# A vision tower's first batch: its mixer is put in front of the class token's set-up

## What is computed

```python
ek = exp(k); ew = exp(w_bias * local_mask)              # token mixer, q, k, v = 1x1 projections of x
y  = sigmoid(q) * (ew @ (ek * v)) / (ew @ ek)
h  = layernorm(y @ out_w + out_b + x) * ln_g + ln_b
h  = concat([cls_tok, h])                               # 257 tokens
W_ = amp * cos(phase)                                   # per q, k, v, o; 32 harmonics, 16 heads of 16
h  = h + holo(attention(layernorm(h)))                  # each projection: (z @ basis.T) @ W_.T
h  = h + ffn(layernorm(h))                              # shared and 8 routed experts, top 2
```

## Time and profile before

| | |
|---|---|
| median of 3 runs (lowest, highest) | 2409.51 us (2408.36, 2416.81) |
| profiled execution: its time, its span | 2408.09 us, 2406.3 us |
| TensorE busy, share of the span | 2203.2 us, 92% |
| VectorE, ScalarE, GpSimd busy | 59%, 42%, 28% |
| mean granted TensorE clock | 0.981 |

### The profile page before, as it was taken

How to read it: one execution, slowest core, us unless ns; L and a number is a source line. 1 busy time by engine, 2 the same in 40 slices (tenths; PEclk the granted TensorE clock), 3 DMA queues, 4 the chain that set the end, 5 groups by cost and what they waited for, 6 DMA issues and landing times. The chain is left out here.

```text
span 2406.3 us, 42478 instructions
## 1 busy us (share of the span) xinstructions
PE 2203.2 (92%) x15647; PEld 1868.9 (78%) x15647; DVE 1413.4 (59%) x3028; ACT 1005.3 (42%) x2074; POOL 683.9 (28%) x734
## 2 busy tenths in 40 slices
PE   3789999999999999999997699999999999999998
PEld 2567677777767677776765599999999888889998
DVE  6356666666666666666664344467664444444666
ACT  0134445454444545444444333322223555554232
POOL 3323323232332323232220211100002333333665
PEclk9799999999999999999999899999999999999999
DMA  2242432323132342424222333300001333333555
GB/s 78 36 66 53 77 58 65 74 49 74 49 81 54 69 69 54 75 48 79 54 54 38 137 119 132 110 27 28 27 27 60 104 104 106 105 104 104 175 174 153
DMA packets 125337, 189.44 MB, mean 79 GB/s; under 512 B 23153, under 2 KB 76418, under 8 KB 125138
## 3 DMA queue, kind: packets, MB, share of 16 engines
q1 hardware_dynamic: 102050, 135.52, 23.9%
q0 software_dynamic: 12736, 34.69, 4.9%
q10 hardware_dynamic: 10352, 16.52, 2.1%
HBM read 84.52 MB, written 49.58 MB: 56 GB/s over the span
## 5 line engine op out<-in xcount | busy, mean ns | idle before, releaser
L799 DVE TENSOR_REDUCE mx<-ps 128x2 f32<-128x514 f32 x512 | 351.1, 686 | 213.4 <-PE ps L455 213.2
L639 ACT ACTIVATE pT<-ps 128x514 f32<-128x514 f32 x512 | 306.6, 600 | 367.4 <-PE ps L472 363.8
L455 PE MATMUL ps<-km,q 112*128 112x258 f32 x1024 | 263.1, 339 | 92.8 <-DVE mx L799 80.7
L455 PEld LDWEIGHTS ps<-km,q 112*128 112x128 f32 x1024 | 162.1, 190 | 189.6 <-DVE mx L799 141.6
L1924 POOL DMA_INDIRECT z<-zd,itab x136 | 129.2, 950 | 484.5 <-DVE itab L1837 268.3
L472 PE MATMUL ps<-q,km 114*128 114x258 f32 x1024 | 226.8, 304 | 7.0 <-ACT pT L639 3.4
L1221 PE MATMUL ps<-zhi,whi 128*128 128x256 f32 x1056 | 218.4, 289 | 4.0 <-DVE wlo L1864 3.9
L1221 PE MATMUL ps<-zhi,wlo 128*128 128x256 f32 x1056 | 214.5, 284 | 0.3 <-issue 0.2
L1221 PE MATMUL ps<-zlo,whi 128*128 128x256 f32 x1056 | 213.8, 284 | 0.4 <-issue 0.4
L1249 ACT ACTIVATE sil<-ps 128x512 f32<-128x512 f32 x132 | 79.0, 598 | 295.3 <-PE ps L1221 237.7
L472 PEld LDWEIGHTS ps<-q,km 114*128 114x128 f32 x1024 | 160.9, 191 | 51.0 <-issue 28.1
(11 more groups left out here) (310 smaller groups left out, 4986.0 us busy)
## 6 DMA issues: line engine op xcount, KB each, us to landing
yd<-raws SPq DMA_DIRECT2D x136, 128.0 KB
q<-qhi SPq DMA_DIRECT2D x128, 129.0 KB, 4.2
km<-khi SPq DMA_DIRECT2D x256, 64.5 KB, 3.3
xs<-in_x SPq DMA_DIRECT2D x64, 256.0 KB, 4.6
z<-hscr SPq DMA_DIRECT2D x46, 256.0 KB
raws<-in_wu SPq DMA_DIRECT2D x12, 768.0 KB, 4.7
hscr<-h SPq DMA_DIRECT2D x34, 256.0 KB, 5.1
zd<-z SPq DMA_DIRECT2D x33, 256.0 KB, 2.1
```

The costliest lines, as they stand in the source:

```text
L455: last = pe.matmul(ps[:, k, 0:NP], q2[p % U][0:MAXROW, QAT[g], t * P:(t + 1) * P], km[p % 2][0:MAXROW, k, g, :], start=True, stop=True)
L639: act.activation(pT[:, 2 * g:2 * g + 2, t, :], ps[:, score_bank(b, n):score_bank(b, n) + 2, 0:N], ACT.Exp, scale=HD ** -0.5).then_inc(s_ok, 1)
L799: dve.tensor_reduce(mx[:, t, 2 * QAT[g]:2 * QAT[g] + 2], ps[:, 0:2, 0:N], AX_X, ALU.max, negate=True).then_inc(mx_ok, 1)
```

## The change

Nothing is computed otherwise; work is put in another order.

- The first five loads (the mixer's weights, of `brow` the 64 rows that are read) get a semaphore of their own, `mix_in`; six more follow on SyncE's queue, and seven are issued by ScalarE after x has come in.
- GpSimd fills `km` without a wait and splits x of batch 0 straight after.
- VectorE makes `mhalf` first, splits the mixer's weights behind three of four `q2` fills, and takes the class token's statistics ahead of the cosine's argument; batch 0's share of step -3 is written out between the pieces of the set-up.
- TensorE does batch 0's mixer first, then the class token's products, then step -2; it waits for `spread_ok` 3, `ones_in` and `vb_in` only after step -2.
- ScalarE does the Exp of the bias and batch 0's gate and exponentials before Sin, and a Tanh of one element (`warm`) ahead of step -2.

```diff
+    warm = sb("warm", [1, 1])
...
-    loads = [(wkv, a["wkv"]), (wq, a["wq"]), (idn, a["idn"]), (brow, a["brow"]), (bq, a["bq"]), (wbT, a["wbT"]), (mskT, a["mskT"]),
-             (outw, a["outw"]), (lng, a["lng"]), (lnb, a["lnb"]), (basT, a["basT"]), (basoT, a["basoT"]),
-             (phs, a["phs"]), (amp, a["amp"]), (bdm, a["bdm"]),
-             (vbdm, a["vbdm"]), (eye, a["eye"]), (clsr, a["clsr"])]
-    LOADED = 16 * len(loads)
+    first_loads = [(wkv, a["wkv"]), (wq, a["wq"]), (idn, a["idn"]), (brow[0:2 * SLOT], a["brow"][0:2 * SLOT]), (bq, a["bq"])]
+    loads = [(mskT, a["mskT"]), (wbT, a["wbT"]), (phs, a["phs"]), (amp, a["amp"]), (outw, a["outw"]), (lng, a["lng"])]
+    more_loads = [(clsr, a["clsr"]), (basT, a["basT"]), (eye, a["eye"]), (bdm, a["bdm"]), (vbdm, a["vbdm"]), (lnb, a["lnb"]),
+                  (basoT, a["basoT"])]
+    FIRST = 16 * len(first_loads)
+    LOADED = 16 * (len(loads) + len(more_loads))
...
@@ SyncE
+        for dst, src in first_loads:
+            sp.dma_start(dst[:], src).then_inc(mix_in, 16)
         for dst, src in loads:
             sp.dma_start(dst[:], src).then_inc(c_load, 16)
...
-        sp.wait_ge(half_ok, 1)
+        sp.wait_ge(half_ok, 2)
         sp.wait_ge(km_set, 2)
...
@@ TensorE, cls_tiles, and its program (the class token's products move down as they are,
@@ but for bank 7 in place of bank 3)
+            if n == 0 and m == 0:
+                pe.wait_ge(spread_ok, 1)
...
-        pe.matmul(ps[0:NH, 3, 0:D], rbc[:], Wz[:, 2, :], start=True,
-                  stop=True).then_inc(clsqkv_ps, 1)
...
+        pe.wait_ge(mixw_ok, 1)
+        mixer_q(0, 0)
+        mixer_kv(0, 0, 0)
+        mixer_kv(0, 0, 1)
         pe.wait_ge(ew_ok, 1)
-        pe.wait_ge(mixw_ok, 1)
-        pe.wait_ge(spread_ok, 2)
+        mixer_sum(0, 0)
+        mixer_sum(0, 1)
+        pe.wait_ge(c_load, LOADED)
+        mixer_out(0, 0, 0)
+        mixer_out(0, 0, 1)
+        pe.wait_ge(c_set, 1)
+        pe.wait_ge(clsz_ok, 1)
...
+        pe.matmul(ps[0:NH, 7, 0:D], rbc[:], Wz[:, 2, :], start=True,
+                  stop=True).then_inc(clsqkv_ps, 1)
+        steps_of(step, -2, -2)
+        pe.wait_ge(spread_ok, 3)
         pe.wait_ge(ones_in, 16 * 2 * 2)
         pe.wait_ge(vb_in, 16 * 3)
-        steps_of(step)
+        steps_of(step, -1)
...
@@ ScalarE
+        act.wait_ge(x_in, 32)
+        for dst, src in more_loads:
+            act.dma_start(dst[:], src).then_inc(c_load, 16)
+        act.wait_ge(wb_ok, 1)
+        act.activation(ewT[:], wbT[:], ACT.Exp).then_inc(ew_ok, 1)
+        act.wait_ge(mixw_ok, 1)
+        mixer_gate(0)
+        mixer_exp(0, 0)
+        mixer_exp(0, 1)
         act.wait_ge(arg_ok, 1)
         act.activation(tr[:], tn[:], ACT.Sin).then_inc(cos_ok, 1)
-        act.wait_ge(wb_ok, 1)
-        act.activation(ewT[:], wbT[:], ACT.Exp).then_inc(ew_ok, 1)
...
-        steps_of(step)
+        mixer_norm(0, 0)
+        act.activation(warm[:], one1[:], ACT.Tanh)
+        steps_of(step, -2)
...
@@ VectorE
+        dve.memset(mhalf[:], -0.5).then_inc(half_ok, 1)
+        dve.memset(oner[:].bitcast(F32), 1.0).then_inc(half_ok, 1)
+        dve.memset(mneg[:], -1.0)
+        dve.memset(one1[:], 1.0)
+        dve.memset(h2[:], 0.0)
+        dve.memset(clso[:], 0.0).then_inc(clso_ok, 1)
+        dve.memset(Wz[:], 0.0)
+        for t in negr:
+            dve.memset(t[0:NH, :].bitcast(F32), 0.0)
+        for t in q2[:3]:
+            dve.memset(t[32:SLOT2, :, :].bitcast(F32), 0.0)
+        dve.wait_ge(mix_in, FIRST)
+        dve.tensor_copy(wqr[:], wq[:])
+        dve.tensor_copy(wkvr[:], wkv[:])
+        dve.tensor_copy(idr[:], idn[:])
+        dve.tensor_scalar(bqh[:], bq[:], 0.5, None, ALU.mult)
+        chain(dve.tensor_copy(browr[:], brow[0:2 * SLOT, :]))
...
+        dve.tensor_tensor(browr[SLOT:2 * SLOT, :], brow[SLOT:2 * SLOT, :], browr[SLOT:2 * SLOT, :],
+                          ALU.subtract).then_inc(mixw_ok, 1)
+        dve.memset(mv3[:, B * LT:, :], 0.0)
+        dve.memset(vbd[:], 0.0)
+        dve.memset(pce[:], 0.0)
+        dve.wait_ge(c_load, LOADED)
         dve.tensor_copy(mskf[:], mskT[:]).then_inc(mask_ok, 1)
+        chain(dve.bn_stats(clsst[:], clsr[:]))
+        chain(dve.bn_aggr(clsmv[:], clsst[:]))
+        dve.tensor_scalar(clsrs[:], clsmv[:, 1:2], EPS, None, ALU.add).then_inc(clsvar_ok, 1)
...
         dve.tensor_scalar(clsz[:], clsr[:], clsmv[:, 0:1], clsrs[:], ALU.subtract, ALU.mult).then_inc(clsz_ok, 1)
+        mixer_ekv(0, 0)
+        mixer_ekv(0, 1)
+        dve.memset(va[0][:], 0.0)
+        chain(dve.memset(va[1][:], 0.0))
+        dve.memset(va[0][:, :, :, HD:HD + 1], 1.0)
+        dve.memset(va[1][:, :, :, HD:HD + 1], 1.0).then_inc(c_set, 1)
+        mixer_inverse(0, 0)
+        mixer_inverse(0, 1)
+        mixer_y(0)
         dve.wait_ge(cos_ok, 1)
...
         dve.tensor_copy(Wz[2 * HARM:3 * HARM, 2, :], W[2 * HARM:3 * HARM, :]).then_inc(w_ok, 1)
+        mixer_stats(0)
         dve.tensor_copy(eyer[:], eye[:])
...
         dve.tensor_copy(rbc[:], rT[:, CLS:N].broadcast_to([3 * HARM, NH])).then_inc(clsr_ok, 1)
+        attn_stats(0, 0)
         dve.wait_ge(clsqkv_ps, 1)
...
-                          bdh[:].rearrange("p a f h -> p (a f h)"), ALU.subtract)
+                          bdh[:].rearrange("p a f h -> p (a f h)"), ALU.subtract).then_inc(spread_ok, 1)
...
+        for t in q2[3:]:
+            dve.memset(t[32:SLOT2, :, :].bitcast(F32), 0.0)
         dve.wait_ge(wo_in, 16 * 3)
...
+        steps_of(step, -2, -2)
         dve.wait_ge(vb_in, 16 * 3)
         dve.memset(tick[:], 0.0).then_inc(spread_ok, 1)
-        steps_of(step)
+        steps_of(step, -1)
...
@@ GpSimd
-        pool.wait_ge(half_ok, 1)
         for t in km:
             pool.memset(t[:].bitcast(F32), 0.0).then_inc(km_set, 1)
+        pool.wait_ge(half_ok, 1)
+        split_x(0, 0)
         pool.wait_ge(mask_ok, 1)
...
         pool.tensor_tensor(clsrs[:], clsrs[:], mhalf[0:1, 0:1], ALU.pow).then_inc(clsrs_ok, 1)
-        split_x(0, 0)
```

## The result

The changed kernel's median is 2390.72 us in 4 runs (2385.45 to 2399.78), beside 2413.16 us (2408.36 to 2418.21, 4 runs) for the kernel before: ratio 0.9913, 95% interval 0.989 to 0.9936. Two later sets on one chip each gave 0.9921 (0.9894 to 0.9949) and 0.9932 (0.9905 to 0.9959). The gain is 21, 19 and 16 us where 26 were forecast; the direction is right, the size a quarter too large by the first set and over a half by the last. The execution profiled took 2399.78 us, its span is 2397.1.

What follows compares the result with a forecast made beforehand. TensorE bounds the steady part, chains between engines the start. Start 27.4 us earlier less y 1.4 late gives a 26.0 gain: 2382.1 against the profiled 2408.09, forecast 2383 us against the median 2409.51, range 2374 to 2392.

Steps and rivals of the forecast that it cites:

- Start of the mixer, 27.4 us earlier: Batch 0's first mixer product starts at 15.4 instead of 42.8 us (bounds 12.8 and 15.6).
- y 1.4 us late, and nothing behind y: VectorE between weights and y, slowed beside GpSimd: y 0.4 to 2.4 us late, taken as 1.4; later work costs 0.
- upper bound for ekv: If all VectorE work from the cosine's argument on waits for GpSimd, ekv begins near 26.2, making y 2.4 us late.
- lighter case: Only VectorE's copies and scalar operations wait for GpSimd: ekv pair at 24.2, y 0.4 us late.
- The moved set-up at no cost: Class token set-up behind the mixer's output: batch 1's first ekv late by 2.7 us at most, cost 0, 5 us slack.
- The table load: One more ScalarE load, 1.28 us, between mixer norm and attention norm: costs 0, or 1.3 if on the path.
- The loads: Loads in time for mask and gate, 1.3 us to spare; a rival had them late, costing 2.5 to 4 at 20 us.
- SyncE and GpSimd kept ahead: Third x asked for near `turn` + 6, split by + 16, before GpSimd's next duty 25.7 us after `turn`: cost 0.
- `turn` to the maxima one for one, then the steady part: `turn` moves from 73.75 to 47.7, and the maxima and steady stages follow by the same 26.0 us.
- The rival of a warm TensorE: TensorE at a higher clock after `turn`, up to 5 us more: gain 34, so 2375 us; chance 0.13.
- the slower one: TensorE enters its steady part at the lower clock, each batch costing about 30 us: 2443 us; chance 0.03.

Runs made afterwards that it cites:

- ekv_first: Changed kernel with VectorE's two batch-0 ekv ahead of the cosine's argument and the `va` fills behind y; median 2390.07 us, ratio 0.9901.
- split_later: Changed kernel with GpSimd waiting for the cosine's argument before it splits x of batch 1; profiled span 2395.9 us.
- after_4: Changed kernel again without an edit, its fourth profile; 7 runs, median 2392.75 us, ratio 0.9932.
- light_start: ekv_first plus light 128-row products, results unread, in TensorE's gaps from the second sum to the end of step -1; median 2390.72 us, ratio 0.9869.

## Why the prediction came out as it did

*Start of the mixer, 27.4 us earlier: right.* 15.36 was measured where 15.4 stood, and for the reason given: the cast ended with GpSimd's subtraction.

*y 1.4 us late, and nothing behind y: the step that failed.* From the first product to `turn` the kernel before needed 30.9 to 31.35 us, the changed one 36.4 to 36.9 in three profiles and 34.6 in a fourth. In the first pair of profiles `turn` was 5.5 us late against the first product, where the sum had 1.4: y itself 3.4 (done at 34.96, 19.6 us after the product, against 16.2), and 2.1 more behind y, where the sum had no term. The wait for GpSimd was foreseen and its upper bound for ekv, 26.2, was all but exact (25.98). What I left out is that `mixer_sum` for the first sum waits for `ekv_ok`: I held ekv only against the second sum and the first sum's own end, and let nothing but the fills and the reciprocals follow from it. With ekv at 26.0 the sum starts at 26.53 instead of 23.2, and y comes as late as the sum; ekv_first and split_later, which take nothing else away, show these 3.4 us. The other 2.1 lie mostly in the products of the mixer's output: its end came 6.5 us after y (39.39 + 2.05 against 34.96), where the prediction used the 4.7 of the kernel before. There, as in after_4, the first four of these products ran at the time of the high clock; in the changed kernel's first profile they did not. The first four in before, after and after_4:

```profile
59.87 1.11 PE L392 MATMUL ps<-outw,rden 128*128 128x256 f32 x4
```

```profile
36.02 2.05 PE L396 MATMUL ps<-outw,rden 128*128 128x256 f32 x4
```

```profile
35.15 1.11 PE L396 MATMUL ps<-outw,rden 128*128 128x256 f32 x4
```

So this part is the clock, and it differs between executions; why it was lower here in three of four profiles is not shown.

*Which operations wait.* The one with one input, L930, waited for GpSimd's cast, as the prediction's lighter case had it. The row of L931, with two SBUF inputs, shows now that such an operation waits too: 3.04 us beside GpSimd's subtraction, 0.43 without. The Trainium skill's rule (SBUF — State Buffer, Who interferes with whom), that a VectorE instruction with two SBUF inputs contends with a GpSimd instruction that reads SBUF, agrees with that row. I had weighed it at half; it should have been taken whole. That alone would have made y 2.4 us late, not the 3.4 measured; the rest is the first sum's wait.

*The moved set-up at no cost: right.* `turn` was released by ScalarE's z, not by the class products; batch 1's first ekv ran at 56.56, 0.6 us after its ek was done, where up to 2.7 was allowed. The table load costs nothing, with the Tanh or without. The loads were in time: the mask's cast ran at 16.24 behind the fill. SyncE and GpSimd kept ahead.

*`turn` to the maxima one for one, then the steady part: right on average, and unsure by the clock.* The mean of the profiles gives 22.8 us at `turn` (74.3 to 51.55) and 21.3 at the last but one sending (1289.1 to 1267.8). Behind that T is anywhere from 69 to 83 us in either kernel. So the profile on which the prediction rests was one with A and T both short; against it the changed kernel seemed to lose 13 us. Between the means of the spans the gain is 16.9 us, so 4 to 5 of the 21.3 are missing at the end, less than T's own spread of 13 in so few profiles. The rival of a warm TensorE did not come true, nor the slower one. The warm one's size, 5 us from `turn` to the maxima, was too large even with fillers: light_start has 24.3 us there against 27.1, and 7.8 less up to the first sending.

*The forecast.* 26.0 less the 4.1 by which the step was short (2.0 in y, 2.1 behind it) is 21.9, the gain of the first pair at `turn` and near the first measured gain of 21; the later sets gave 19 and 16. The range of 2374 to 2392 held the first median of 2390.72. It was reckoned from a median of 2409.51 for the kernel before, which in the result is 2413.16; as a ratio the range is 0.9853 to 0.9927, which holds the first two sets, while the last, 0.9932, lies just outside.

*Left open:* why T came out short in one of four profiles of the changed kernel and in two of three of the kernel before, whether that is chance or the change's doing, and with it part of the difference between the three measured gains; and which property of a product (rows, values) raises or holds the clock.

## What to carry to other kernels

When a part is moved behind a contended stretch, list every wait of its readers in the code before calling a delay covered: here one `wait_ge` turned slack into 3.4 us. Put the operations that the chain reads (ekv) in front of those that only a later stage needs (the argument), and keep GpSimd's long instructions out of the stretch in which VectorE is the chain, since moving GpSimd first gave 3.4 of its 5.65 us back. Profile the kernel before more than once: two stretches whose length depends on the clock shifted its marks by up to 20 us with no edit.

## What the runs showed of the hardware

One VectorE operation of 0.43 us took 3.04 beside a GpSimd instruction, and a cast of 0.29 took 2.94; both ended within 0.3 us of GpSimd's end. An operation with one SBUF input did the same beside GpSimd's cast, 2.70 us instead of 0.29. After 17 us of unbroken 64-row products TensorE was at the 1.2 GHz level, by the durations, for some 12 us of the mixer's products behind them, while 74 light 128-row ones in the gaps of the tail held 2.4 GHz where it had fallen: T at a mean clock of 0.96 instead of 0.66. And the same instructions of the tail took 69 to 83 us by their mean clock of 0.91 to 0.66, some 13 of the 30 us between the shortest and the longest of 28 runs of the kernel before on one chip (2398.65 to 2428.5).
